# New slot orders for five engines and new counts of constant matmuls in a two-stream transformer kernel

## The reference, cut to what matters

```
x = x_in[b]                                    # 256 x 128
h = layernorm(x)*(1+ca)+sa;  x = x + ga * L0_attn(h)     # index scores, top-k 96 keys, latent attention, 8 heads
h = layernorm(x)*(1+cb)+sb;  x = x + gb * L0_ffn(h)      # 2 x (window attention 64, 8 heads + gated MLP 341)
h = layernorm(x)*(1+ca')+sa'; x = x + ga' * L1_attn(h)   # 16 heads of 8, full attention
h = layernorm(x)*(1+cb')+sb'; x = x + gb' * L1_ffn(h)    # 16 experts, top 8, and a shared one
```

## Time and profile before

| what | before |
|---|---|
| median of 3 runs | 1548.83 us (1548.13 to 1551.87) |
| the profiled execution | 1548.75 us |
| its span | 1547.0 us |
| mean granted TensorE clock | 0.967 |
| PE busy | 1349.1 us (87%), 11615 matmul records |
| DVE busy, ACT busy | 916.5 us (59%), 912.3 us (59%) |
| POOL busy | 319.1 us (21%) |

### The profile page before, as it was taken

The page is one execution under the profiler, slowest core; times in us unless marked ns, Lnnn a source line. Parts: engine busy times, 40 slices in busy tenths (PEclk is TensorE's granted clock), DMA queues, the critical chain, the costliest instruction groups (busy, mean ns, idle before and its releaser), DMA issues. The chain is left out here.

```text
span 1547.0 us, 30139 instructions
## 1 busy us (share of the span) xinstructions
PE 1349.1 (87%) x11615; PEld 951.3 (61%) x11615; DVE 916.5 (59%) x3062; ACT 912.3 (59%) x2270; POOL 319.1 (21%) x420
## 2 busy tenths in 40 slices
PE   7789899899898888987987989888998799898797
PEld 5555656576666556665765665655676466566575
DVE  3755675746465757565456667576455665766633
ACT  3444766566744657656864375754775436765576
POOL 0511030111332212210153103020024310302002
PEclk9889999999999999999998999999999799999999
DMA  7120000000102100000011200000001210000000
GB/s 273 48 66 21 14 1 1 1 5 5 45 21 57 28 5 1 1 1 5 4 46 30 63 17 2 1 1 1 4 4 46 72 24 14 1 1 1 1 1 8
DMA packets 41871, 36.42 MB, mean 24 GB/s; under 512 B 31296, under 2 KB 35840, under 8 KB 40192
## 3 DMA queue, kind: packets, MB, share of 16 engines
q1 hardware_dynamic: 41728, 34.49, 7.7%
HBM read 25.46 MB, written 7.44 MB: 21 GB/s over the span
## 5 line engine op out<-in xcount | busy, mean ns | idle before, releaser
L1105 ACT ACTIVATE arena<-ps 128x512 f32<-128x512 f32 (+7 forms) x560 | 255.0, 488 | 229.9 <-PE ps L587 28.7
L546 PE MATMUL ps<-mean_mat 128*128 128x256 bf16 x1773 | 275.1, 287 | 7.7 <-DVE arena L1460 4.1
L546 PEld LDWEIGHTS ps<-mean_mat 128*128 128x128 bf16 x1773 | 167.2, 102 | 104.8 <-issue 63.0
L1876 POOL TENSOR_TENSOR arena<-arena 128x512 f32<-128x512 f32 x64 | 81.3, 1272 | 456.3 <-DVE arena L1473 456.2
L1301 ACT ACTIVATE arena<-arena,small 128x192 f32<-128x192 f32 (+1 forms) x256 | 129.8, 510 | 37.8 <-DVE small L1653 37.5
L1754 DVE TENSOR_TENSOR arena<-arena,ps 128x512 f32<-128x512 f32 x64 | 41.9, 685 | 78.9 <-ACT arena L1391 71.9
L1250 ACT ACTIVATE arena<-arena,small 128x224 f32<-128x224 f32 (+1 forms) x128 | 56.6, 443 | 53.8 <-DVE small L1609 53.5
L1701 DVE TENSOR_REDUCE small<-ps 128x4 f32<-128x1024 f32 x64 | 75.3, 1218 | 19.5 <-PE ps L988 19.3
L1590 DVE TENSOR_TENSOR gath<-ps,rank_tab 96x512 f32<-96x512 f32 x96 | 62.9, 683 | 36.5 <-PE ps L574 36.2
L1453 DVE CUSTOM_DVE_ANT_0 arena<-ps,mask_w_bf 128x192 f32<-128x192 f32 (+1 forms) x256 | 67.4, 319 | 20.9 <-PE ps L660 20.6
L1350 ACT ACTIVATE arena<-ps 128x512 f32<-128x512 f32 x128 | 66.0, 602 | 22.6 <-PE ps L1022 22.6
(11 more groups left out here) (284 smaller groups left out, 2956.3 us busy)
## 6 DMA issues: line engine op xcount, KB each, us to landing
idxb<-idx_scratch SPq DMA_DIRECT2D x8, 1536.0 KB, 6.4
score_scratch<-arena SPq DMA_DIRECT2D x24, 256.0 KB
w_experts<-in_experts SPq DMA_DIRECT2D x3, 1088.0 KB, 16.7
w_wqkv<-in_wqkv SPq DMA_DIRECT2D x1, 1536.0 KB, 9.0
arena<-score_scratch SPq DMA_DIRECT2D x96, 16.0 KB, 2.1
arena<-arena SPq DMA_DIRECT2D x96, 16.0 KB, 1.8
arena<-in_x SPq DMA_DIRECT2D x8, 128.0 KB, 3.3
out_x<-arena SPq DMA_DIRECT2D x8, 128.0 KB, 1.9
```

The lines of the kernel that those rows point to most:

```text
L546: mm(to, still[:, 0:P], still, start=True, stop=True)
L1105: return act.activation(dst, src, ACT.Copy)
L1876: ins = pool.tensor_tensor(own, own, turned, ALU.add)
```

## The change

The five strings of `TURNS` and the two of `BUSY` are replaced. Nothing else is: the instructions apart from the fillers, the waits and the buffers stay, and each stream's own order of slots too. The slot orders and the counts were made anew from durations at the full clock of TensorE.

```
 TURNS = {
-    "pe": ("51311111234223414111111111212111311111112111211111111111222211111111211111122111111211122111111112121121121111"
...
+    "pe": ("41211144114122413221111111212111112111111141111111111111211112111111112111111221111211111221111111121211211211"
...
-    "sp": ("117111612682212111416612151651532111212142126118511172151238751851174233943525af3312121411568212i515132521c111"
...
+    "sp": ("016162121141242111571123111611241161937e3132465214331122g1163131141111121121141211k321512121c72716332111832712"
...
-BUSY = [("70389000008c45784400023000075521452014424b424c168500016002472010b41238c287295080309c957341210200100050c0040002"
...
+BUSY = [("b093c95209a796c1bb711200103540334000490098101a44b8a0201340706750711404c2681c100107b016b83800080911017b4c056303"
...
```

More of the change, by code:

```diff
@@ L102 @@
 TURNS = {
[L103 to L122, removed]
+    "pe": ("41211144114122413221111111212111112111111141111111111111211112111111112111111221111211111221111111121211211211"
+            "11111111312111133511112211231223112112121111112111112121123111111111131222111111111131111212111111221111221212"
+            "12121113111111111111113111111111113122113231122222111112431123211111112221112111111211111112221111111111211112"
+            "22111111221111221112131212121211211111113111111111112111111131112112212111111112112113112211111111112132211111"
+            "1211112112121111111111211111111211111122111122111213121113121121111111311211121311161"),
@@ new lines @@
+    "act": ("41325211111371211112112142111121111111114111111111112111111211111111211211112111153121111113221221111124116111"
+            "13122421122521112223221121211111311111122111111111121212221111111131111211121112321111221632241211421111211111"
+            "11112121221111312111211213123221111121133221221111211111121111111222112211112112112211222211211231172971112111"
+            "1111111121111111311121214732211111111111541121121121111112111212321111221121111112111112322222121a213243312112"
+            "111213111214"),
@@ new lines @@
+    "dve": ("41216211112111138521211131222111111141111111111132111112111111112111122111121111121137631111111111477731211111"
+            "24131221111332111132312221111112231111121112211131111212111112222111121212121113131331113111111141111111212111"
+            "11431232122112112111221211211111123111211112332213212211211111111111121123212311121212131513627213211121312131"
+            "13213313122332321111112121112111111112113312111122111121112322111111112212111213111312113551111123132215"),
@@ new lines @@
+    "pool": ("018121434114125231149561212122663511211161232221283322133314432233112212221114741411121311a52127412b3124323111"
+            "11111122143211125135319151311814128114161392213731231213112551113134221212127111712138121111211179222211223113"
+            "4126215112147147121114121646314119114214832221111314411313"),
+    "sp": ("016162121141242111571123111611241161937e3132465214331122g1163131141111121121141211k321512121c72716332111832712"
+            "1617122131511123131314141223111111111262312413145464a2343125141714216111111142141217524141111312123314114d1932"
+            "41715212431315b11c55263136a1"),
@@ L134, in slot_order @@
     return order
[L137 to L142, removed]
+BUSY = [("b093c95209a796c1bb711200103540334000490098101a44b8a0201340706750711404c2681c100107b016b83800080911017b4c056303"
+         "14b2490810610202024046340026a40101160472000ac3c948c202420314a1675112320240ac102408c001000682a01106613305020c08"
+         "000136382622883006206b408412803001c144750200510331069418751023450000"),
+        ("b3160551448380c9308003120209210010210030c6723b827733011466337c394540a0020302bc00036a2174b31244201309ccbc113001"
+         "102023294bc2c216200c6538166707c006416070721809bca802a001715135a5062101234412003415a822010b30815c01212473180122"
+         "1c00041c07bc100001002247324c024a011045408820716105220a14a31073000113")]
 GATHERED = ["gscore_mm", "gathT_mm"]
```

## The result

The changed kernel takes 1584.78 us (median of 4 runs, 1582.3 to 1589.78), against 1548.48 us before. The ratio is 1.0224 with a 95% interval of 1.0200 to 1.0247, about 35 us. The forecast was 1542 us, and 1584.78 lies above its range.

What follows compares the result with a forecast made beforehand. The prediction took engine-to-engine latency, not one engine, as the bound. Fillers +10, clock -6, start -1, SP round 3 -2, SP round 0 +1 and orders -9 gave -7 us from 1548.75, so 1542 us, range 1522 to 1562.

Steps and rivals of the forecast that it cites:

- What bounds the kernel: Whole kernel: no single engine is the bound; it is engine-to-engine latency and how two streams fill each other's waits.
- More fillers, +10: PE: 333 more fillers, 36.3 us of issue, partly hidden in idle time, add 10 us (bounds 0 and +19.6).
- The share of fillers on the chain: Last quarter: 54% of filler time lies on the chain that ended last, an upper bound of its cost.
- My sign of being wrong: PE's busy time rises by 36 us and idle falls by less: fillers have then only lengthened the span.
- The clock, -6: PE's half-speed stretches: denser fillers recover a third of 18 us, so -6 us (bounds 0 and -18).
- the start, -1: Kernel start: added fillers cost 0.1 us and the clock may rise sooner, -1 us (bounds +1 and -5).
- SP, round 3, -2: SP in round 3: stream 1's input load and indices go earlier, -2 us (bounds -8 and 0).
- SP, round 0, +1: SP in round 0: third score piece issued 4.3 us later, stream 1's spread sooner, +1 us (bounds +4.3 and -4).
- The orders of PE, ACT and DVE, -9: Moved slots on these engines: an order from true durations removes more waits than it makes, -9 us.
- The bound of 15 us: Engine orders: a tenth of 163 us of PE waits for ACT, DVE and POOL, bounding gain and loss.
- The experts' steps, nothing: Experts' steps: same order as before, price and cover unchanged, no term in the sum.
- The slower one: Rival: new fillers stand in the chain's way, 1548.75 + 18 = 1567 us; chance 0.24.

Runs made afterwards that it cites:

- the three additive stretches: Kernel before with the change's orders only in round 0, only in rounds 1 and 2, or only in round 3: 1.0083, 1.0105 and 1.0043.
- w1: Kernel before; on SP in round 0 stream 1's two index DMAs go ahead of stream 0's third score piece, their spread stays behind it: 1.0014.
- w4: Kernel before; on DVE in round 0 stream 1's top-k stands ahead of stream 0's gather evacuations, as in the change: 0.9982.
- x1: Slot orders of before with the 2106 fillers of the change: 1.0030 against the kernel before.
- x2: Slot orders of the change with the 1773 fillers of before: 1.0224 against the kernel before.
- y3: The changed kernel with SP's order of before: 1.0166 against the kernel before.
- w3: Kernel before with SP's order of the change from round 3 on: 0.9982.
- y2: Kernel before with SP's order of the change in round 0 only, stream 1's index DMAs and spread ahead of stream 0's third score piece: 1.0058.
- E5: Not a run: a slot in each stream's order that waits for PE's expert matmuls; it has no time of its own.
- v1: Kernel before with one ACT inversion of the change: at the end of round 1 stream 0's E5 stands ahead of two slots of stream 1: 1.0016.
- w2: Kernel before with one DVE inversion of the change: in the last round stream 0's E5 stands ahead of stream 1's routing: 1.0031.
- v2: The change with three places as before, SP in round 0, ACT at the end of round 1, DVE in the last round: 1.0117 against the kernel before.

## Why the prediction was wrong, point by point

*What bounds the kernel.* The reading of a chain of latencies from engine to engine held. It should have made me more careful: what one stretch lost, nothing later took back, as the three additive stretches show. That does not hold for every single delay; those of 1.9 and 2.1 us in w1 and w4 left nothing in the time that can be told.

*More fillers, +10.* Too high. The counts cost 0.3%, 5 us, on the old orders and nothing that can be told on their own. The share of fillers on the chain was an upper bound, and I took half of it. My sign of being wrong came, busy time up by 24.5 us and idle time up too, but what I had said that it means, that the fillers have only lengthened the span, is excluded by x1 and x2.

*The clock, -6, and the start, -1.* I had expected a mean of 0.975 and 6 us for it. The new counts come near to that on the old orders, 0.973 in x1, and win no time. The new orders take it back: 0.956 to 0.970 in the change. A part of that lies in the wait for the scores, 33.1 in place of 20.6 us at line 608. It is not all: y3, where line 608 waits 21.0 us again, still shows 0.956 to 0.966, and what holds the clock down there is open. In the window from 84 to 118 us, in which the longest of these waits lies, the granted clock was 0.80 before and is 0.65 in the changed kernel:

```profile
84.00:118.00 34.00, 18.82 (x141) 13.50 (x134) 11.76 (x51) 11.63 (x43) 8.10 (x12) 0.65 0.24 70
```

By the Trainium skill (TensorE: Matmul & The Clock Gate, "HAM oscillation — how this bites in real kernels") a wait for a DMA sends the clock down, and the cure is an order in which PE does not run into it; the trace agrees for this window, by its 0.65 and 0.80. At the start the step was right, the fillers cost nothing and the clock rose sooner.

*SP, round 3, -2.* Size and sign agree with w3 (-2.8, interval -6 to 0).

*SP, round 0, +1.* This step failed. It measured +9.0 (interval +4 to +14), where my bound was +4.3. The late issue was sized about right, 3.8 us for 4.3. What the sum left out is the spread's own transfer: 1536 KB now went out 0.37 us ahead of the 256 KB piece, and the piece, which stands in line behind it, takes 8.9 in place of 5.8 us. The rows had it. The input load behind the same kind of spread took 7.76 us, I read that rightly as a place in a queue, and in round 3 I counted it as a gain; in round 0, where SP's move puts a piece into just that place, I did not count it as a cost. I then took a value below the issue's own price because stream 1's spread came sooner, and no run shows a gain from that: y2, which has it, measures +9.0 us, and w1, which does not, +2.

*The orders of PE, ACT and DVE, -9.* This step failed, and by the most. y3, the change with SP's order of before, measures +25.7 (interval +15 to +37), and the stretches without SP's moves in rounds 0 and 3 give 16.3 + (12.9 - 9.0) + (6.7 + 2.8) = 30. POOL's order, which I had not named, is in both. The bound of 15 us on the side of loss was wrong as well. It scaled idle time that existed by the share of moved slots of PE, where the two inversions that were tried are on ACT and DVE, with twice as many moved slots (133 and 142 outside the longest common sequence). And it took the sign from a belief, that an order from true durations must be better. No row said so. The 54% on the chain spoke of the old counts, which were indeed improved, and not of the old orders.

*The experts' steps, nothing.* I wrote that they have the same order as before and keep their price, with their cover unchanged. Within one stream that is so, but between the streams E5 had changed places on ACT at the end of round 1 and on DVE in the last round. These are the inversions of v1 and w2, +2.5 and +4.8 us.

*The rivals.* The slower one had the right sign and half of the size, +18 us against +36, for a reason that x1 and x2 exclude. The one that was missing is that a single inversion on DVE or ACT costs 2 to 5 us, and that there are many of them; w2 shows one, and for the many no run does.

**What stays open.** About 18 us of the loss, all but what v2 gave back, are localized in stretches but not traced to moves, most of them in rounds 1 and 2. Both inversions that were tried look as if the order had counted on PE's expert matmuls being done sooner than they are. That would fit durations at full clock, but it was not tried with an order made from other durations, and a planner that does not let one DMA stand in line behind another could have made the third. This is argued, not shown.

## What to carry to other kernels

When several in-order queues carry two interleaved streams, look at each inversion for what stands behind the slot that waits; adding idle time by shares of moved slots says nothing. A large DMA that is moved ahead of a small urgent one has to be priced twice, for the time until the issuing engine comes to the small one and for the time that the large one's bytes take, behind which the small one stands in line. Cut a large reordering where all engines have done the same slots and time the pieces: here they were additive, and three single moves gave back nearly half of the loss. Do not take a step between two single traces for the cost of an edit: 10 us arose between them where nothing was changed.

## What the runs showed of the hardware

A DMA of 256 KB took 5.8 us from issue until SP could issue what waits for it, and 8.9 us with the 1.5 MB spread issued 0.37 us ahead of it (y2; 9.0 in the change). None of its packets started before the last one of the spread had (98.63 against 98.17 us in y2, 102.16 against 101.85 in the change). 193 us of constant matmuls on PE lift the mean granted clock from 0.895 to 0.967, and that is worth about 10 of 1550 us; 333 more lift it to 0.973 (x1, mean of 10 executions, 0.969 to 0.977) and cost 0.3%.
